# A twelve-layer decoder on one core: head centring moved into the weights of the memory attention, its value bias into the output bias, its lengths and transposes taken by half of the batches

## The reference, cut to what matters

```
def _ln(t, w, b):                      # over the 16 numbers of a head
    m = jnp.mean(t, axis=-1, keepdims=True)
    v = jnp.var(t, axis=-1, keepdims=True)
    return (t - m) * jax.lax.rsqrt(v + 1e-6) * w + b

y_dca, y_main = y[:, -16:, :], y[:, :-16, :]
kv_dca = (y_dca @ Wkv_dca + bkv_dca).reshape(b, 16, 2, 16, 16)
k_dca, v_dca = _ln(kv_dca[:, :, 0], kn_dca_w, kn_dca_b), kv_dca[:, :, 1]
q = _ln((x @ Wq + bq).reshape(b, s1, 16, 16), qn_w, qn_b)
k = _ln((y_main @ Wk + bk) by heads, kn_w, kn_b);  v = (y_main @ Wv + bv) by heads
ctx = softmax(q k^T / 4) v  +  softmax(q k_dca^T / 4) v_dca        # two softmaxes, added
x = x + ctx @ Wo + bo
```

## Time and profile before

| what | us |
|---|---|
| median of 3 runs | 1915.83 |
| the profiled execution | 1914.34 |
| its span, first to last instruction | 1912.4 |
| stage of linear attention, within the span | 861.3 to 924.5 |
| stage of memory attention, within the span | 924.5 to 1047.8 |
| projections of that stage on PE | 930.6 to 958.5 |
| from there to the first scores | 958.5 to 975.3 |

### The profile page before, as it was taken

How to read it: one execution, slowest core, us unless ns; L and a number is a source line. 1 busy time by engine, 2 the same in 40 slices (tenths; PEclk the granted TensorE clock), 3 DMA queues, 4 the chain that set the end, 5 groups by cost and what they waited for, 6 DMA issues and landing times. The chain is left out here.

```text
span 1912.4 us, 37176 instructions
## 1 busy us (share of the span) xinstructions
PE 1681.9 (88%) x13787; PEld 1302.4 (68%) x13790; DVE 1187.0 (62%) x2333; ACT 924.3 (48%) x1956; POOL 445.3 (23%) x497
## 2 busy tenths in 40 slices
PE   7978856789999789976878869999999988999898
PEld 4767723558888646643667747777777766888676
DVE  3676688656666512226655678888888874666522
ACT  2445566246666411112255456666667644555432
POOL 2020011023333032221300224455545430000200
PEclk9989977899999989998979989999999989999899
DMA  2020001200100272221000000101100012110000
GB/s 101 3 91 3 4 30 47 97 18 26 30 28 25 76 307 45 45 50 43 14 2 23 22 17 26 31 28 28 30 26 32 26 33 107 34 33 25 1 1 22
DMA packets 27679, 77.84 MB, mean 41 GB/s; under 512 B 2992, under 2 KB 14896, under 8 KB 25392
## 3 DMA queue, kind: packets, MB, share of 16 engines
q1 hardware_dynamic: 23488, 71.17, 10.9%
q0 software_dynamic: 4080, 5.13, 1.7%
HBM read 63.01 MB, written 13.28 MB: 40 GB/s over the span
## 5 line engine op out<-in xcount | busy, mean ns | idle before, releaser
L2528 DVE SCALAR_TENSOR_TENSOR arena<-bank,arena 128x508 f32<-128x508 f32 (+2 forms) x204 | 151.6, 744 | 28.4 <-ACT arena L2524 16.4
L2654 PE MATMUL bank<-L3a_wo,L3a_y_gated 128*128 128x256 f32 x512 | 124.1, 387 | 0.0
L2883 DVE TENSOR_TENSOR L3a_decays<-L3a_decays,L3a_cb_masked 128x512 f32<-128x512 f32 x128 | 95.0, 805 | 43.5 <-ACT L3a_decays L2766 43.5
L225 PE MATMUL bank<-const 128*128 128x512 f32 (+1 forms) x156 | 78.0, 633 | 41.9 <-PEq L65 41.9
L2766 ACT ACTIVATE L3a_decays<-bank 128x512 f32<-128x512 f32 x128 | 66.1, 604 | 97.6 <-PE bank L2628 97.6
L2681 PE MATMUL bank<-L3a_xnT_high,L3a_w_high 128*128 128x512 f32 x256 | 106.4, 416 | 1.5 <-ACT L3a_decays L2766 1.5
L2654 PEld LDWEIGHTS bank<-L3a_wo,L3a_y_gated 128*128 128x128 f32 x512 | 92.4, 190 | 17.7 <-issue 7.3
L2681 PE MATMUL bank<-L3a_xnT_high,L3a_w_low 128*128 128x512 f32 x256 | 100.3, 392 | 0.0
L2681 PE MATMUL bank<-L3a_xnT_low,L3a_w_high 128*128 128x512 f32 x256 | 100.2, 391 | 0.0
L1932 PE MATMUL bank<-L1f_experts,xnT 128*128 x184 | 86.0, 611 | 0.9 <-DVE xnT L2035 0.7
L2980 POOL TENSOR_TENSOR arena<-arena 128x1024 f32<-128x1024 f32 x32 | 81.1, 2535 | 14.8 <-ACT arena L2773 14.8
(11 more groups left out here) (609 smaller groups left out, 4668.7 us busy)
## 6 DMA issues: line engine op xcount, KB each, us to landing
arena<-in_L3p SPq DMA_DIRECT2D x32, 388.0 KB, 3.0
L1f_experts<-in_L1f SPq DMA_DIRECT2D x8, 1536.0 KB, 17.0
arena<-in_L1x SPq DMA_DIRECT2D x18, 384.0 KB, 3.0
arena<-in_L3x SPq DMA_DIRECT2D x18, 384.0 KB, 3.1
arena<-in_L0f SPq DMA_DIRECT2D x1, 4224.0 KB, 13.0
arena<-in_L3f SPq DMA_DIRECT2D x1, 4055.0 KB, 12.2
rows_sent<-L1a_blank SPq DMA_DIRECT2D x1, 2967.0 KB, 11.5
xnT<-rows_sent SPq DMA_DIRECT2D x23, 129.0 KB, 2.1
```

Of the source, the lines that this page charges most:

```text
L225: self.nc.tensor.matmul(self.k.ps[bank][:, 0:width], self.k.ident, self.k.const[:, 0:width], start=True, stop=True)
L2528: return nc.vector.scalar_tensor_tensor(dst[:, :, d:], psum[:, :, 0:P - d], wcol, dst[:, :, d:], ALU.mult, ALU.add)
L2654: mm = nc.tensor.matmul(ps[g // 2][:, (g % 2) * C:(g % 2 + 1) * C], yg[:, o, g * P:(g + 1) * P], wo[:, o, :], start=False, stop=False, ski ...
L2883: nc.vector.tensor_tensor(d, d, cbm[:, 4 * half:4 * half + 4, :].rearrange("p b t -> p (b t)"), ALU.mult).then_inc(S["dec_ready"], 1)
```

## The change

1. The stage ahead centres the weights. The image of the memory attention is laid out anew, so that `wq`, `wk`, `wkd` and the bias `bqk` stand first (CENTRED = 1536 columns, 96 heads of 16). In `l2_attn` DVE sums each head of these (one reduction of 128x1536), POOL divides by 16 and subtracts. Queries and keys then come out centred, and L2322, L2323 and L2324 go.
2. The value bias goes with the output weights. POOL adds the two value biases and spreads them to a block, PE multiplies it with `wo` (two products), DVE adds `bo`, and POOL adds the result to x. The eight L2256 go, and with them 512 columns of the image (4 come in).
3. Lengths and turns by halves. Mean of squares, reciprocal and root are taken for batches 0 to 3 and 4 to 7 apart; products of early batches stand between the later projections. The transposes of half 0 stay ahead of half 1, and DVE writes `qT` where ACT did.

```diff
 # l2_attn, POOL and DVE
+                pool.wait_ge(s_means, 1)
+                nc.gpsimd.tensor_scalar(means[:, :], means[:, :], 1.0 / 16, None, ALU.mult).then_inc(s_means, 1)
+                pool.wait_ge(s_means, 2)
+                nc.gpsimd.tensor_tensor(heads, heads, along(means[:, :], 16), ALU.subtract).then_inc(s_means, 1)
...
+                dve.wait_ge(k.after.s_img, 16)
+                nc.vector.tensor_reduce(means[:, :], heads, AX.X, ALU.add).then_inc(s_means, 1)
                 dve.wait_ge(s_den, 1)
 # l2_xattn, PE
+                pe.wait_ge(s_bv, 2)
+                for c in range(KC):
+                    mm = nc.tensor.matmul(ps[4][:, 0:C], bvT[:, c, :], wo[:, c, :], start=(c == 0), stop=(c == KC - 1))
+                mm.then_inc(s_bop, 1)
...
-                    nc.tensor.matmul(vb[:, :], k.ident, w["bvs"], start=True, stop=False, skip_group_check=True)
...
+                pe.wait_ge(s_bo, 1)
+                turns(0)
+                pe.wait_ge(s_in, 2)
+                pe.wait_ge(s_qin, 2)
+                turns(1)
                 pe.wait_ge(s_vin, NB)
                 a.scores(pe, 0)
-                pe.wait_ge(s_in, 8)
+                pe.wait_ge(s_in, 4)
+                pe.wait_ge(s_qin, 4)
 # ACT
+                def lengths(half):
+                    t = slice(4 * half, 4 * half + 4)
+                    act.wait_ge(s_var, half + 1)
+                    nc.scalar.activation(rstd[:, t, :], var[:, t, :], ACT.Sqrt).then_inc(s_rstd, 1)
...
+                    if b == 4:
+                        lengths(0)
                 for half in range(2):
...
+                        ins.then_inc(s_in, 1)
+                        if half == 0 and c == 0:
+                            lengths(1)
 # DVE
                 for b in range(NB):
                     dve.wait_ge(s_qk, b + 1)
+                    nc.vector.tensor_tensor(qk[:, b, :], ps[b % 2][:, :], w["bqk"], ALU.add).then_inc(s_cent, 1)
                     if b:
+                        squared(b - 1)
+                    if b >= 5:
+                        normalised(b - 5)
+                squared(NB - 1)
+                normalised(3)
+                for b in range(4, NB):
+                    normalised(b)
+                queries(0)
+                queries(1)
 # POOL
+                pool.wait_ge(s_w, 16)
+                nc.gpsimd.tensor_tensor(bv[:, :], w["bv"][:, 0:KC], w["bv"][:, KC:2 * KC], ALU.add).then_inc(s_bv, 1)
+                pool.wait_ge(s_bv, 1)
+                nc.gpsimd.tensor_tensor(bvT[:, :, :], along(bv[:, :], P),
+                                        k.c["zero"].unsqueeze(2).to_broadcast([P, KC, P]), ALU.add).then_inc(s_bv, 1)
```

More of the change, by code:

```diff
@@ L2081, in l2_attn @@
             "kv_summed", "decay_ready", "decays_set", "numerators", "reciprocals", "spread", "den_logs"))
+        heads = k.after.img[:, 0:CENTRED].rearrange("p (h d) -> p h d", d=16)
+        means, s_means = st.sb("head_means", [P, CENTRED // 16]), st.sem("weights_centred")
         ln = Norm(k, st)
@@ L2243, in _, with turns @@
                 pe.wait_ge(s_w, 16)
+                pe.wait_ge(s_bv, 2)
+                for c in range(KC):
+                    mm = nc.tensor.matmul(ps[4][:, 0:C], bvT[:, c, :], wo[:, c, :], start=(c == 0), stop=(c == KC - 1))
+                mm.then_inc(s_bop, 1)
                 pe.wait_ge(s_ctx, 4)
+                def turns(half):
+                    for m in range(2):
+                        for c in range(KC):
+                            for j in range(4):
+                                b = 4 * half + j
+                                pe.wait_ge(s_ln, b + 1)
+                                mm = nc.tensor.transpose(ps[4 + 2 * m + c][:, j * P:(j + 1) * P],
+                                                         qk[:, b, m * C + c * P:m * C + (c + 1) * P], k.ident)
+                            mm.then_inc(s_t, 1)
                 for b in range(NB):
                     if b >= 2:
-                        pe.wait_ge(s_read, b - 1)
+                        pe.wait_ge(s_cent, b - 1)
                         pe.wait_ge(s_vin, b - 1)
@@ new lines, in normalised, with queries @@
+                def normalised(b):
+                    dve.wait_ge(s_rstd, b // 4 + 1)
+                    nc.vector.tensor_tensor(by_head(qk, b, hd), by_head(qk, b, hd), along(rstd[:, b, :], hd),
+                                            ALU.mult).then_inc(s_ln, 1)
+                def queries(half):
+                    own = slice(half * HALF, (half + 1) * HALF)
+                    for c in range(KC):
+                        dve.wait_ge(s_t, 4 * half + c + 1)
+                        nc.vector.tensor_scalar(a.qT[:, c, own], ps[4 + c][:, :], w["nw"][:, 0:1], w["nb"][:, 0:1],
+                                                ALU.mult, ALU.add).then_inc(s_qin, 1)
@@ L2332, in _ @@
-                dve.wait_ge(s_sqread, NB - 1)
-                step(nc.vector.tensor_scalar(var[:, :, :], var[:, :, :], 1.0 / hd, 1e-6, ALU.mult, ALU.add))
-                nc.vector.reciprocal(var[:, :, :], var[:, :, :]).then_inc(s_var, 1)
-                dve.wait_ge(s_rstd, 1)
-                for b in range(NB):
-                    h3 = qk[:, b, :].rearrange("p (h d) -> p h d", d=hd)
-                    nc.vector.tensor_tensor(h3, h3, along(rstd[:, b, :], hd), ALU.mult).then_inc(s_ln, 1)
+                    nc.vector.tensor_tensor(qk[:, b, :], ps[b % 2][:, :], w["bqk"], ALU.add).then_inc(s_cent, 1)
```

85 lines of the change are left out of this document (35 added, 50 removed).

## The result

The changed kernel takes 1902.77 us (median of 5 runs, 1899.38 to 1905.83), the kernel before 1915.75 on the same chip (5 runs, 1913.10 to 1916.07). The direction was right. The profiled execution took 1902.77 us as well, with a span of 1901.0.

What follows compares the result with a forecast made beforehand. PE was taken to bound the projections, a chain of handovers the turns. The terms -6.9 + 0.9 + 0.1 + 0 - 0.9 = -6.8 us took 1915.83 to 1909.0 us, 8-in-10 range 1906 to 1912.

Steps and rivals of the forecast that it cites:

- Projections, -6.9 + 0.9 + 0.1 = -5.9: Projections: value bias off PE -6.9 us, two output-weight products +0.9, wait at batch 2 against normalisation gain +0.1.
- the wait at batch 2: In the projections, PE waits until ACT has read batch 0's value bank: +0.3 us.
- The normalisation: Ahead of the projections: DVE's L189 no longer lies beside POOL's copy, up to 0.43 us comes back.
- Centring in the stage ahead, 0: Stage ahead: DVE's sum and POOL's subtraction fit into idle time, cost 0 us; bounds 0 and 1.6.
- Turns, -0.9: Last projection to first scores, done by halves: 15.9 us instead of 16.8, -0.9; bounds +1.7 and -4.
- rival A: Turns: PE keeps the full clock of 2.4 GHz, up to 3 us more gained, 1906; chance 0.13.
- Behind the scores, 0: After first scores: DVE's half 1 queries and ACT's keys finish in time for L418, as before; no term in the sum.
- the forecast of -6.8: Sum over projections, normalisation, stage ahead and turns: -6.8 us, giving a median of 1909.0 us.
- Both stretches lie on the path; what they lose moves every later stage as a whole.: Projections and turns: time lost there shifts all later stages as a whole, with no term for those stages.
- Rival D: Attention and later stages move against the clock: slower, +13.6 us to 1922 with eight more half-clock stretches; chance 0.03.
- The three runs agree within 0.3 us: Whole kernel before: agreement of three runs within 0.3 us, cited against Rival D.
- The likeliest case: Whole kernel: 1909.0 us, own range 1907.5 to 1910.5; chance 0.61.

Runs made afterwards that it cites:

- the bias alone: Kernel before with only the value bias carried by the output weights, centring and turns as before; 1911.22 us, ratio 0.9979.
- the centring alone: Kernel before with only the centring moved to the stage ahead, value bias and turns as before; 1909.99 us, ratio 0.9981.
- the delays: Kernel before with POOL zeroing four or seven pieces of finished `v` at the memory-attention stage's end; 1912.42 us (ratio 0.9999) and 1916.25 us (1.0007).
- the early root alone: Changed kernel with the second half's root moved ahead of ACT's keys of the first half; 1900.69 us, ratio 0.9935.
- the fed kernel: Changed kernel with the second root moved ahead of ACT's first-half keys, plus 11 unused products on constants on TensorE; 1898.38 us, again 1900.80 us.

## Why the prediction was wrong in size and right in kind

Point by point, in the order of the prediction. The traces compared first are the second ones of both kernels, which show the same clock in the untouched stages ahead of the change.

- **Projections, -6.9 + 0.9 + 0.1 = -5.9.** Right. They end 27.94 us into the stage instead of 33.95, so -6.0. The two products took 0.94, the wait at batch 2 was 0.18. The normalisation gave 0.43 of its own, as said.
- **Centring in the stage ahead, 0.** Right, 63.12 became 63.22. That it must go to free DVE was right as well: the bias alone lost 3.6 us to DVE.
- **Turns, -0.9.** Exact in the first trace (15.9 forecast, 15.91 measured), -1.8 in the second, where thirteen transposes ran partly at 2.4 GHz. This is a small part of rival A: the transposes behind the last projection sometimes meet the full clock. In none of the changed kernel's traces did it hold through the turns.
- **Behind the scores, 0.** The scores and the first pass were taken as before. From the first scores to L418 it was 5.09 us and is 4.22, and the pass behind it 7.94 and 9.14: -0.9 and +1.2. The products are the same, and the clock is not. With -6.0 and -1.8 this makes the -7.5 of the stage.
- **The stage as a whole.** -7.5 us in the second pair of traces and -5.1 in the first (118.19 against 123.27), where the normalisation ran at the lower clock. The mean, -6.3, is near the forecast of -6.8, which lies between the two; that the mean comes so near is in part luck, since two executions of the changed kernel differ by 2.4 us in this stage.
- **"Both stretches lie on the path; what they lose moves every later stage as a whole."** This is the sentence that failed. The sum put nothing on the stages behind. They did not move as a whole: they became 2.4 to 2.6 us shorter, with 47.2 us at 1.2 GHz in place of 57.4. All five traces of kernels without the bias products and without a delay or products on constants show it, the kernel before in neither of its two. Rival D knew that the later stages could move against the clock, and priced it in one direction only, as a loss. The row that should have warned was among: 2 us at 0.50 with TensorE full, out of a stretch of 3.4, which rival D itself priced at 1.7 us. Such stretches also lie behind the stage, and the table above has from 47 to 62 us of them.
- **The range.** "The three runs agree within 0.3 us" was taken as the scatter of the kernel. Eighty executions of it, over all comparisons here, lie between 1906.9 and 1919.4, and eleven of the changed kernel between 1897.8 and 1905.8. The likeliest case's own range of plus or minus 1.5 us was narrower than the scatter of the thing that it forecast.

So the sum is -6.3 in the stage and -2.5 behind it, -8.8, against a difference of the medians of 11 to 13. The remaining 2 to 4 us are not settled. In the traces they lie ahead of the change, in code that both kernels have: 1.2 us in the second pair, and 3.95 in the first, where the execution of the changed kernel had 116.1 us at 1.2 GHz ahead of the stage and the other three traces of the two kernels 133.1. The kernel before with a delay, which is the kernel before up to there, had 116.1, 105.8 and 133.1 in its three traces, so such executions come without the change as well.

The recorded executions give a second estimate. The time follows the mean clock: of 75 executions of the kernel before, the 24 with 0.945 lie between 1914.0 and 1915.9 us, the five with 0.951 between 1910.1 and 1910.6. A straight line through the 75 falls by 0.83 us for 0.001. The eleven of the changed kernel lie 8.2 us below it, and the other 3.1 of the 11.3 us between the means go with a higher mean clock (0.9506 against 0.9469). By the same line the centring alone is worth 0.5 us, and the delays cost 0.9 and 2.6 us, about their own length. Why the changed kernel meets the higher clock more often, as a whole, stays open.

The Trainium skill ("TensorE: Matmul & The Clock Gate", section "HAM oscillation — how this bites in real kernels") describes a kernel whose pauses drop TensorE to the lower clock again and again. The traces here agree as to the kind: the turns, with idles of 2.46 and 5.45 us, had a mean of 0.71, and with products on constants in the idle times at 1.00.

## What to carry to other kernels

Before forecasting a change of a few microseconds, look in the windows for stretches in which TensorE is full at half clock, in the changed stage and in all the stages behind it: each can come or go with a shift of a microsecond (8.5 against 9.2 us in the table above made 2.6 us), so the price of a shift is its length plus or minus such stretches, and the range must hold both signs. Measure the scatter on a dozen executions, not three. Where an engine is relieved, look who would be next and relieve it in the same step, and where TensorE waits in a chain of handovers, try products that nobody uses: here they shortened their stage by 4.6 to 5.5 us beside the early root alone, and lost 1.2 to 2.7 of it behind.

## What the runs showed of the hardware that was not expected

- In one trace a delay of 1.2 us at one barrier was given back in full by unchanged code behind it (1.24 against -1.3); one of 2.6 us cost 0.7 more in one trace and 2.9 in another. The sum behind the barrier went with the place at which the clock fell, in fourteen traces of ten kernels.
- The unchanged self attention of block 1, far ahead of the change, lasted 69.0 us in some executions and 66.3 in others, of both kernels.
- DVE's four normalising products (L147) slowed when POOL's copies moved beside them. They took 1.40 us before:

```profile
926.85 0.60 DVE L189 SCALAR_TENSOR_TENSOR ln_bias<-ln_mv,ln_rstd 128x8 f32<-128x8 f32 x1
927.37 1.40 DVE L147 TENSOR_SCALAR xn<-x,ln_mv,ln_rstd 128x256 f32<-128x256 f32 x4
```

and 2.19 in the changed kernel (921.94 above), while L189 ahead of them fell from 0.60 to 0.17. POOL's copy (0.98 us from 922.35) lies beside L147 now and lay beside L189 then. TensorE's first projection did not come later by it: the normalisation as a whole was 0.43 us shorter in the second trace. The Trainium skill ("SBUF — State Buffer", section "SBUF: two separate sides") has a lock between the two engines, held for whole instructions, against DVE instructions with two SBUF inputs and against those with one that run in a mode of two ports. L189 has two inputs and agrees with it (0.60 and 0.17); L147 reads one tensor, and its 2.19 against 1.40 would fit the second kind, but no row shows its mode.
- Sixteen transposes of 128x128 took 3.65 us at 1.2 GHz (961.73 above) and 1.97 at 2.4 (961.49 in the fed kernel), 0.23 and 0.12 each.
- POOL's product of 128x1536 with a broadcast operand took 2.81 us, hardly more than the 1024 wide one beside it (2.34), and the 96 wide multiplication between them 0.47 with 0.1 us of gap on either side.
